# A split second layer for nine feed-forward tiles between two batches, with the rounding on ScalarE and the subtraction on GpSimd

## The reference

```
logits = z @ gate_w.T + gate_b
logits = logits * rsqrt(mean(logits**2) + eps) * rms_w
gates  = softmax(logits / 0.5);  g = max gate;  norm_g = g / (g + 1e-6)
h = gelu(einsum('nd,edh->neh', z, w1) + b1)
y = einsum('neh,ehd->ned', h, w2) + b2
out = x + (y * norm_g).sum over experts
```

## Time and profile before

| | us |
|---|---|
| median of 3 runs (305.35 to 305.57) | 305.56 |
| the profiled execution | 304.81 |
| its span | 303.1 |
| PE busy in the span | 285.4 (94%) |
| DVE / ACT / POOL busy | 205.6 / 187.8 / 90.1 |
| share of the chain that ended last: PE / DVE / ACT / POOL | 69% / 20% / 2% / 3% |

### The profile page before, as it was taken

The page is one execution under the profiler, slowest core; times in us unless marked ns, Lnnn a source line. Parts: engine busy times, 40 slices in busy tenths (PEclk is TensorE's granted clock), DMA queues, the critical chain, the costliest instruction groups (busy, mean ns, idle before and its releaser), DMA issues.

```text
span 303.1 us, 5329 instructions
## 1 busy us (share of the span) xinstructions
PE 285.4 (94%) x1671; PEld 181.7 (60%) x1672; DVE 205.6 (68%) x829; ACT 187.8 (62%) x292; POOL 90.1 (30%) x213
## 2 busy tenths in 40 slices
PE   7887989999879999999999999999999999998995
PEld 2533654664557675757576667666566664656882
DVE  5788787887868684646768784648776831267882
ACT  6780625764467396857486396857396887535443
POOL 1459203602322155020430264020400241700070
PEclk9998999999999999999999999999999999999999
DMA  6541060401200041013000150011001000000101
GB/s 186 187 128 44 2 208 4 135 27 42 83 4 0 3 121 49 2 24 99 1 5 0 43 160 3 2 42 50 0 3 39 1 4 0 0 3 0 35 0 35
DMA packets 12827, 13.47 MB, mean 44 GB/s; under 512 B 2240, under 2 KB 9280, under 8 KB 12544
## 3 DMA queue, kind: packets, MB, share of 16 engines
q1 hardware_dynamic: 11660, 11.95, 12.7%
q0 software_dynamic: 1024, 1.05, 1.7%
q10 hardware_dynamic: 116, 0.14, 0.2%
HBM read 5.40 MB, written 1.05 MB: 21 GB/s over the span
## 4 chain that ended last, share of the span: by engine, by line
PE 69%; DVE 20%; issue 4%; POOL 3%; ACT 2%; ACTq 1%; DVEq 1%; POOLq 0%
DVE unused L1219 12%; PE ffn_bank L960 11%; PE v_ring L836 9%; PE pv_bank L892 8%; PE a_ring L858 8%; PE a_ring L775 6%; PE a_ring L777 5%; PE a_ring L776 5%; PE a_ring L870 2%; PE ffn_bank L783 2%; PE ffn_bank L973 1%; DVE z L1119 1%; PE v_ring L843 1%; PE ffn_bank L974 1%; PE ffn_bank L975 1%
## 5 line engine op out<-in xcount | busy, mean ns | idle before, releaser
L1219 DVE CUSTOM_DVE_ANT_0 unused<-v_ring,cst 128x256 bf16<-128x256 f32 (+3 forms) x256 | 111.7, 487 | 42.7 <-PE v_ring L836 37.6
L629 ACT ACTIVATE probs<-a_ring 128x512 f32<-128x512 f32 x160 | 87.2, 599 | 66.5 <-PE a_ring L870 41.4
L836 PE MATMUL v_ring<-k_stack,q_stack 128*128 128x512 f32 (+1 forms) x176 | 81.1, 490 | 3.6 <-DVE row_max L1219 1.8
L858 PE MATMUL a_ring<-q_stack,k_stack 128*128 128x512 f32 (+3 forms) x256 | 63.4, 329 | 0.3 <-ACT probs L629 0.3
L647 ACT ACTIVATE hidden<-a_ring,cols_sb 128x512 f32<-128x512 f32 x64 | 43.2, 688 | 29.3 <-PE a_ring L777 29.1
L858 PEld LDWEIGHTS a_ring<-q_stack,k_stack 128*128 128x128 f32 x256 | 45.2, 192 | 13.1 <-issue 5.5
L960 PE MATMUL ffn_bank<-hidden,w_sb 128*128 128x512 f32 x100 | 51.3, 598 | 0.0
L836 PEld LDWEIGHTS v_ring<-k_stack,q_stack 128*128 128x128 f32 x176 | 33.0, 193 | 23.7 <-issue 10.8
L892 PE MATMUL pv_bank<-probs,v_ones 128*32 128x256 f32 (+3 forms) x512 | 42.1, 440 | 0.0
L546 POOL TENSOR_SCALAR_AFFINE_SELECT probs<-probs 128x512 f32<-128x512 f32 x16 | 10.1, 632 | 101.2 <-ACT probs L629 101.2
L775 PE MATMUL a_ring<-zT_hi,w_hi 128*128 128x512 f32 x64 | 28.3, 443 | 0.8 <-DVEq L1105 0.8
(11 more groups left out here) (137 smaller groups left out, 348.1 us busy)
## 6 DMA issues: line engine op xcount, KB each, us to landing
k_stack<-k_hi SPq DMA_DIRECT2D x60, 32.0 KB
q_stack<-q_hi SPq DMA_DIRECT2D x6, 256.0 KB
hidden<-w SPq DMA_DIRECT2D x1, 1024.0 KB, 8.5
k_stack<-k_lo POOLq DMA_DIRECT2D x32, 32.0 KB, 2.2
x_res<-x SPq DMA_DIRECT2D x4, 256.0 KB, 2.9
w_sb<-w SPq DMA_DIRECT2D x1, 1024.0 KB, 5.7
x_in<-x SPq DMA_DIRECT2D x3, 256.0 KB, 3.1
q_stack<-q_lo SPq DMA_DIRECT2D x3, 256.0 KB
```

Source lines behind the costliest of these rows:

```text
L629: act.activation(probs[:, n % 2, quads[0]:quads[-1] + 1, KIND_AT[kind]:KIND_AT[kind] + cols], a_bank()[:, 0:len(quads) * cols].rearrange(" ...
L836: pe.matmul(dst, q_stack[b % 2][:, s, n * P:(n + 1) * P], k_stack[:, s, quads[0]:quads[-1] + 1, 0:cols], start=True, stop=True).then_inc(v ...
L858: last = pe.matmul(dst[:, at:at + P * (TB - j)], k_stack[:, s, q, j * P:(j + 1) * P], q_stack[b % 2][:, s, j * P:T], start=(at == 0), stop ...
L1219: ins = dve.tensor_tensor_reduce(unused[:, (uses[0] - 1) % V_BANKS, at:at + cols], bank_[:, at:at + cols], cst[:, C_MASK + T - cols:C_MASK ...
```

## The change

`LAST_TILES` becomes (2, 2, 3): the last set takes three tiles instead of four, and nine are left for the end. For these nine the second layer is three fp32r products. ACT, behind each gelu, copies the tile to `hidden_hi` (`high_tile`); POOL subtracts it to `hidden_lo` (`low_tile`); PE's `ffn2_middle` follows three tiles behind `ffn1` instead of two. POOL's split of w2 stands behind the mask of the last set and waits for the first two sets' scores of the last batch only. `transpose_z` stands behind the last `ffn1` and ahead of the last three second layers. `split_hidden` waits for the ring from its first tile on.

```
-LAST_TILES = (2, 2, 4)
+LAST_TILES = (2, 2, 3)
...
+            def low_tile(m):
+
+                n = NT * (B - 2) + m
+                pool.wait_ge(high_ready, m - sum(LAST_TILES) + 1)
+                pool.tensor_tensor(hidden_lo[:, m % SPLIT_RING, :], hidden[:, n % HB, :],
+                                   hidden_hi[:, m % SPLIT_RING, :].bitcast(F32), ALU.subtract).then_inc(low_ready, 1)
...
-            pool.wait_ge(e_filled, UNITS * SETS * B)
-            pool.wait_ge(w2_loaded, 16)
-            split(w2_sb[:].rearrange("p n c -> p (n c)"), w2_hi, w2_lo, w2_split, 0)
+                    if b == B - 1 and s == SETS - 1:
+                        pool.wait_ge(w2_loaded, 16)
+                        pool.wait_ge(e_filled, UNITS * (SETS * b + 2))
+                        split(w2_sb[:].rearrange("p n c -> p (n c)"), w2_hi, w2_lo, w2_split, 0)
+            for m in range(sum(LAST_TILES), NT):
+                low_tile(m)
             norm_logits(B - 1)
...
+            def high_tile(m):
+
+                n = NT * (B - 2) + m
+                act.wait_ge(g_freed, n + 1)
+                if m == sum(LAST_TILES):
+                    act.wait_ge(e_filled, UNITS * SETS * B)
+                if m >= sum(LAST_TILES) + SPLIT_RING:
+                    act.wait_ge(ffn2_done, n - SPLIT_RING + 1)
+                act.activation(hidden_hi[:, m % SPLIT_RING, :], hidden[:, n % HB, :], ACT.Copy).then_inc(high_ready, 1)
...
             for m in range(sum(LAST_TILES), NT):
                 gelu_tile(B - 2, m)
+                high_tile(m)
...
+            def ffn2_middle(m):
+
+                pe.wait_ge(w2_split, 2)
+                pe.wait_ge(low_ready, m - sum(LAST_TILES) + 1)
+                cols, i = slice(m * C, (m + 1) * C), m % SPLIT_RING
+                pe.matmul(ffn_bank[:], w2_hi[:, cols], hidden_hi[:, i, :], start=False, stop=False)
+                pe.matmul(ffn_bank[:], w2_lo[:, cols], hidden_hi[:, i, :], start=False, stop=False)
+                pe.matmul(ffn_bank[:], w2_hi[:, cols], hidden_lo[:, i, :], start=False,
                           stop=(m == NT - 1)).then_inc(ffn2_done, 1)
...
                 ffn1(B - 2, m)
-                if i >= 2:
-                    ffn2(B - 2, m - 2)
+                if i >= 3:
+                    ffn2_middle(m - 3)
                 if i == 1:
                     transpose_y(B - 1, 1)
                 if i == 2:
                     transpose_y_norm(B - 1)
                 if i == 3:
                     project_y(B - 1)
-            ffn2(B - 2, NT - 2)
-            transpose_z(B - 1)
-            ffn2(B - 2, NT - 1)
+                if i == len(tiles) - 1:
+                    transpose_z(B - 1)
+            for m in range(NT - 3, NT):
+                ffn2_middle(m)
...
                 dve.wait_ge(g_freed, n + 1)
-                if m >= SPLIT_RING:
-                    dve.wait_ge(ffn2_done, n - SPLIT_RING + 1)
+                dve.wait_ge(ffn2_done, n - SPLIT_RING + 1)
```

More of the change, by code:

```diff
@@ L264, in block_kernel @@
         w2_split = sem("w2_split")
+        high_ready = sem("high_ready")
+        low_ready = sem("low_ready")
         hidden_split = sem("hidden_split")
@@ L961, in ffn2 @@
                           stop=(m == NT - 1)).then_inc(ffn2_done, 1)
+            def ffn2_middle(m):
[5 more added lines that the diff above has]
+                pe.matmul(ffn_bank[:], w2_hi[:, cols], hidden_lo[:, i, :], start=False,
+                          stop=(m == NT - 1)).then_inc(ffn2_done, 1)
             def ffn2_tail(m):
```

## The result

The changed kernel takes 310.12 us (309.45 to 310.71, four runs) against 305.46 us of the kernel before (305.30 to 305.57, four runs): a ratio of 1.0153, 95% interval 1.012 to 1.0187. Forecast were 309.05 and a range of 306.2 to 310.6. The profiled execution took 309.45 us, with a span of 307.7 us, 4.6 more than before.

What follows compares the result with a forecast made beforehand. PE was taken as the bound, with two DVE steps at the seam between batches. −1.56 us (last set), +3.8 (end stage) and +1.25 (clock) gave 3.5 us slower than 305.56: 309.05 us, range 306.2 to 310.6.

Steps and rivals of the forecast that it cites:

- One tile fewer: Last set before the end stage: one tile's first layer (0.70 us) and second layer (0.86) leave the path, 1.56 us gained.
- S: Start of PE's first product of the end stage, at 258.13 us before the change, forecast at 256.57.
- A tile's path: End stage: gelu, ACT's rounding, POOL's subtraction, three products; a tile takes 1.27 us on ACT, 1.28 POOL, 1.40 PE.
- The early split of w2: POOL's split ends near 258.9 us, costing PE nothing; DVE's gates' product may be held, at most 0.2 us lost.
- The hold: POOL's subtractions block DVE's two-SBUF-tensor operations in z's root, two per gap; z at 273.7 us, 3.7 us idle PE.
- The clock: PE's granted clock halves after its idle wait for z; 1.25 us taken, bounds 0 and 1.6.
- F0: Fourth batch's first second-layer product on PE, at 274.10 us before the change, forecast at 277.6.
- (A): Rival: z's short root operations are not held, z in time, 1.0 us faster, 304.55 us; chance 0.13.
- (B): Rival: only the root's three products are held, z at 271.1, 0.35 us faster, 305.2 us; chance 0.04.
- (C): Rival: the hold as summed, but PE's clock kept, 307.8 us; chance 0.26.
- (D): Rival: the hold with one POOL turn less and PE's clock kept, 306.4 us; chance 0.10.
- (E): Rival: only 0.70 us leaves the last set; with one operation to a gap 0.8 more; 310 to 311 us, chance 0.07.

## Why the prediction was right

*One tile fewer.* Right, to the digit: S is at 257.24, which is 258.13 − 1.56 + the 0.67 that were there before (from POOL's mask to S 16.66 us instead of 18.22).

*A tile's path.* Right. From the first gelu's start (259.29 in the trace) its subtraction starts 1.43 us later (1.46 summed), and the products 2.87 later (2.82). PE set the pace with 1.39 to 1.40 a tile.

*The early split of w2.* Right in the hold that was said of it: the gates' product stood until 259.58. It cost 0.15 us of PE's wait (bound 0.2), and the experiment with the late product shows that it is covered.

*The hold.* Right as a mechanism: the experiments with the root in PSUM and with plain fp32 each take it away and bring the 5 us back. Right in its form too: two operations to a gap, five turns of POOL. The open bound (combinations of two SBUF tensors held or not) is at its upper end: three of the five held rows are such combinations. Undersized by 0.3: z's transposition came 17.53 us behind S, where 17.23 were summed. The step that fell short is the list of what is held. I counted the nine operations with two SBUF tensors; the root's first, with one, was held too, for 1.19 us, so that the five turns began earlier in the chain and two operations were left behind the fifth (273.02 and 273.22), where the sum had none; they cost 0.4 us.

The Trainium skill (VectorE: DVE Perf Modes, Mode 2×_2P) says that a tensor_scalar from SBUF to SBUF may use both read ports for its one tensor. The Trainium skill (SBUF — State Buffer, Who interferes with whom) says that in such a mode it contends with GpSimd. The runs agree on the contention: the root's first operation and the normalisation are held beside subtractions (1.19 and 3.25 us), operations of this kind are held for less beside settings to zero (0.46 for the root's second, 1.45 for the normalisation), and the root's first is not held once its result goes to PSUM (0.17). The Trainium skill (SBUF — State Buffer, Who interferes with whom) also says that two SBUF inputs contend with a GpSimd instruction that reads SBUF, not with one that only writes it. The runs agree with both halves: 1.13 to 1.17 us beside subtractions, 0.16 beside settings to zero.

*The clock.* Right that it falls; 1.5 us by the experiment that keeps PE at work, where 1.25 were taken and 1.6 was the bound. Two readings were short. The fall in the earlier trace rows was read as 3.2 us, while its shares of 0.90 and 0.89 give 3.4 (27.8 to 31.2), and in the changed kernel it is 3.4 again. And part of it was to fall into the idle time, but it began at 274.7, as PE's wait ended (274.77).

*The sum.* +3.5 was forecast, +4.64 came in the profiled execution. Of the 1.1 us between, 0.3 are the hold, 0.3 the clock, and 0.67 what lies ahead of the last set, which no term had: the prediction carried that over from one execution, and it varies. Behind F0 0.17 came off. The distance of the forecast from the median depends on this part too, which is luck either way.

*The rivals.* (A) fell: z was 3.83 us late. (B) fell with the combinations. (C) and (D) fell with the clock and with the fifth turn. (E) fell: 1.56 us left the last set, and two operations went to a gap. By its time alone (E) could not be told from what happened: it was priced at 310 to 311, and the median is 310.12. Only the rows part them.

## What to carry over

A cheap operation can be dear when it stands on a serial chain beside a busy POOL. In this kernel an operation of DVE on two SBUF tensors, or a tensor_scalar from SBUF to SBUF, waited for the end of POOL's subtraction, and 0.16 or 0.17 us became 1.1 to 1.2; behind a longer POOL operation 0.16 became 4.2. Before work is given to an idle POOL, look at which DVE chain runs in that stretch and whether it is short serial operations; one operand in PSUM freed them here. And what is queued on PE behind a wait should be what needs it: three products that did not need z stood behind it here, and the idle time cost 1.5 us more by the clock.

## What the runs showed that was not expected

A tensor_scalar from SBUF to SBUF is held too, though it reads one tensor; one is even held by a POOL that only writes (0.46 us instead of 0.17). Its duration gives no sign of it: the root's first takes 0.17 us with its result in SBUF and with its result in PSUM. The part ahead of the change moves the end by 0.67 us between the two profiled executions, in step with the time at which the clock falls there. Runs of one kernel spread over 3 us (304.17 to 307.23 for the kernel before the change, 31 runs), as much as the effects looked for: S to F1 in the trace tells kernels apart that the medians don't.
